# A gated cross-attention block with a SwiGLU layer: the softmax's division moves in front of the turn, onto VectorE, and the loads change order

## What is computed

```python
x = x + tanh(g_xattn[0]) * xattn(ctx, layernorm(x), mask, b)   # 8 heads of 32
x = x + tanh(g_ffn[0]) * ffn(layernorm(x), w_gate, w_up, w_down)

def xattn(memory, query, seq_mask, b):
    Q = split_heads(query) * 32 ** -0.5
    K, V = split_heads(memory[..., :256]), split_heads(memory[..., 256:])
    logits = Q @ K.T + b[0] + -1e30 * (1 - mask)
    return softmax(logits) @ V

def ffn(x, wg, wu, wd):        # weights divided by 127; hidden size 768
    return (silu(x @ wg.T) * (x @ wu.T)) @ wd.T
```

## Time and profile before

| what | value |
|---|---|
| median of 3 runs (lowest, highest) | 141.6 us (140.57, 143.15) |
| span of the profiled execution | 139.7 us |
| PE busy in the span | 129.5 us, 93% |
| DVE busy in the span | 103.4 us, 74% |
| ACT, POOL busy | 90.7 us, 100.3 us |

### The profile page before, as it was taken

One profiled execution on the slowest core, in us unless ns is written; L12 is line 12 of the kernel. 1 busy time (PEld: TensorE's weight loads), 2 busy tenths in 40 slices (PEclk: granted clock), 3 DMA queues, 4 the chain that ended last, 5 costly groups with the idle time before them and its releaser, 6 DMA issues.

```text
span 139.7 us, 3761 instructions
## 1 busy us (share of the span) xinstructions
PE 129.5 (93%) x1276; PEld 98.0 (70%) x1276; DVE 103.4 (74%) x273; ACT 90.7 (65%) x204; POOL 100.3 (72%) x179
## 2 busy tenths in 40 slices
PE   7974998987999999999999999999999999999990
PEld 2324664564566897689779985997667988988870
DVE  4949799977678469787888849878546996676622
ACT  3314599799488877875964889674992556851610
POOL 7463995999999798787788492554697999761530
PEclk9999599999999999999999999999999999999999
DMA  4579990499968930030199106000041062020222
GB/s 139 164 223 359 388 304 9 88 199 195 144 121 155 127 75 0 5 75 5 38 207 195 21 0 150 5 0 0 0 42 38 5 153 77 2 77 2 75 82 89
DMA packets 32033, 14.08 MB, mean 101 GB/s; under 512 B 25588, under 2 KB 31240, under 8 KB 32008
## 3 DMA queue, kind: packets, MB, share of 16 engines
q1 hardware_dynamic: 31968, 13.77, 42.9%
q10 hardware_dynamic: 40, 0.01, 0.1%
HBM read 5.52 MB, written 2.10 MB: 55 GB/s over the span
## 4 chain that ended last, share of the span: by engine, by line
PE 71%; POOL 9%; DMA 7%; DVE 6%; issue 2%; SPq 2%; ACT 0%; POOLq 0%; ACTq 0%; DVEq 0%
PE ps L1426 31%; PE ps L1452 15%; PE ps L1352 4%; DMA x_sb<-in_x_dram 4%; PE ps L1358 4%; PE ps L1328 3%; PE ps L1330 3%; PE ps L1372 3%; PE ps L1283 3%; DMA n_t<-norm 2%; DVE max_cols L1076 2%; POOL rstd L635 2%; POOL q_parts L664 2%; DVE stats L936 2%; PE ps L1212 2%
## 5 line engine op out<-in xcount | busy, mean ns | idle before, releaser
L1426 PE MATMUL ps<-n_t,w_gu_t 128*128 128x256 f16 x384 | 47.7, 273 | 0.5 <-DMA n_t<-norm 0.5
L1426 PEld LDWEIGHTS ps<-n_t,w_gu_t 128*128 128x128 f16 x384 | 36.6, 98 | 6.7 <-DVE h L1131 1.6
L681 POOL TENSOR_TENSOR h<-h 128x256 f16<-128x256 f32 x48 | 31.5, 674 | 11.2 <-ACT h L843 11.2
L1120 DVE SCALAR_TENSOR_TENSOR gated<-tanh_h,ps 128x256 f32<-128x256 f32 x48 | 20.0, 416 | 13.7 <-ACT tanh_h L834 13.5
L834 ACT ACTIVATE tanh_h<-ps 128x256 f32<-128x256 f32 x48 | 18.4, 384 | 15.2 <-PE ps L1426 15.1
L1452 PE MATMUL ps<-w_d_t,h 128*128 128x256 f16 x192 | 24.9, 273 | 0.0
L786 ACT ACTIVATE probs<-ps,exp_bias 128x512 f32<-128x512 f32 x32 | 21.6, 689 | 4.5 <-PE ps L1330 4.1
L1076 DVE TENSOR_REDUCE max_cols<-ps 128x4 f16<-128x512 f32 x32 | 20.7, 683 | 3.8 <-PE ps L1283 3.0
L1131 DVE SCALAR_TENSOR_TENSOR h<-ps,gated 128x256 f32<-128x256 f32 x48 | 20.4, 424 | 2.0 <-DVE gated L1120 0.4
L843 ACT ACTIVATE h<-h 128x256 f16<-128x256 f32 x48 | 18.6, 412 | 2.6 <-DVE h L1131 2.3
L1452 PEld LDWEIGHTS ps<-w_d_t,h 128*128 128x128 f16 x192 | 18.3, 98 | 2.8 <-issue 0.8
(11 more groups left out here) (100 smaller groups left out, 187.3 us busy)
## 6 DMA issues: line engine op xcount, KB each, us to landing
x_sb<-in_x_dram SPq DMA_DIRECT2D x8, 256.0 KB, 8.8
out_dram<-x_sb SPq DMA_DIRECT2D x8, 256.0 KB, 2.3
kv<-in_ctx_dram SPq DMA_DIRECT2D x4, 256.0 KB, 6.5
w_raw<-in_L_ffn_w_gate_dram SPq DMA_DIRECT2D x1, 768.0 KB, 7.8
w_raw<-in_L_ffn_w_up_dram SPq DMA_DIRECT2D x1, 768.0 KB, 9.4
w_raw<-in_L_ffn_w_down_dram SPq DMA_DIRECT2D x1, 768.0 KB, 8.1
q_stacks<-q_parts SPq DMA_TRANSPOSE x12, 3.4
n_t<-norm SPq DMA_TRANSPOSE x7, 3.1
```

Source lines behind the costliest of these rows:

```text
L681: pool.tensor_tensor(h16[:, r % 2, m, 1, :], h32[:, n % NHB, :], h16[:, r % 2, m, 0, :], ALU.subtract).then_inc(h_low, 1)
L1120: mine(dve.scalar_tensor_tensor(out=gated[:, n % 2, :], in0=tanh_h[:, n % 2, :], scalar=1.0, in1=got[:, 0:SH], op0=ALU.add, op1=ALU.mult))
L1426: ins = pe.matmul(dst, lhs, rhs, start=(w == 0 and (k, l) == terms[0]), stop=(k, l) == terms[-1], skip_group_check=True)
```

## The change

Six things are changed together.

1. `wd` multiplies by a 128x32 block of ones instead of `sum_cols`: each head's sum then stands in all 32 rows of its head, one region for one group at a time. `sum_cols` and the POOL instructions that make it go.
2. `oc` moves from ACT to DVE. For each group: a reciprocal of the 128x256 sums, read from PSUM, and a multiplication of the 128x256 values in PSUM with it into `o_sb`, which now holds quotients. `wo` of the next group waits for the multiplication.
3. `at` turns two blocks instead of three; DVE multiplies the turned block by the gate and adds it to `x_sb` in one operation. The reciprocal of 8, the `attn` buffer and the POOL addition go.
4. `var_eps` and `neg_mean` move from POOL to DVE; the statistics of the halves (2,3), (4,5), (6,7) are taken as pairs in the first normalisation.
5. Loads: `x` of the halves 2 and 3 is started before the gates and the weights, and the other loads are mixed differently. Two of three clearing instructions at DVE's start move into the wide program, and two of the small operations for the `exp` bias move to ACT.
6. All five lists of `ORDER` are written anew.

```diff
-        qn2 wn0 qn3 wn1 wn2 nn0 qn4 qn5 nn1 nn2 qn6 fi0 nn3 qn7 nn4 fi1 nn5 nn6 fi2 fi3 fi4 fi5 fi6 fi7""",
+        qn2 qn3 wn0 wn1 nn0 wn2 qn4 nn1 qn5 nn2 nn3 qn6 qn7 nn4 nn5 fi0 fi1 nn6 fi2 fi3 fi4 fi5 fi6 fi7""",
...
-        o_sb = sb("o_sb", [P, 2, NG + 1, SH], F32)
+        o_sb = sb("o_sb", [P, 2, NG, SH], F32)
-        ones32 = sb("ones32", [P, 1], F32)
-        sum_cols = sb("sum_cols", [P, NG, DH], F32)
+        ones32 = sb("ones32", [P, DH], F32)
-        recip = sb("recip", [P, 2, NH], F32)
+        recip = sb("recip", [P, 2, SH], F32)
...
             load_x(sp, 1)
+            load_x(sp, 2)
             load_kv(sp, 1)
+            load_x(sp, 3)
             for n, g in enumerate((g_xattn, g_ffn, attn_b)):
...
-                    elif kind == "attn_t":
-                        n = plan.nth[step]
-                        t = step[1] * QT + step[2]
-                        pool.wait_ge(*plan.emptied(step))
-                        pool.tensor_tensor(x_sb[:, t, :], x_sb[:, t, :], attn[:, n % 2, :],
-                                           ALU.add).then_inc(x1_ready, 1)
...
+                        if which == 2 or norm1_on_pool((step[0].replace("stats", "norm1"), r)):
+                            mine(dve.tensor_scalar(neg_mean[:, at, :], mv[:, at, :, 0], -1.0, None, ALU.mult))
+                        dve.tensor_scalar(var_eps[:, at, :], mv[:, at, :, 1], LN_EPS,
+                                          1.0 / Q_SCALE_SQ if which == 1 else 1.0, ALU.add, ALU.mult
+                                          ).then_inc(var_ready, 1)
...
                     elif kind == "attn_t":
+                        t = step[1] * QT + step[2]
+                        dve.wait_ge(work_filled, plan.filled(step))
+                        dve.scalar_tensor_tensor(out=x_sb[:, t, :], in0=bank32(plan.bank(step))[:, 0:D],
+                                                 scalar=tanh_g[:, 0:1], in1=x_sb[:, t, :],
+                                                 op0=ALU.mult, op1=ALU.add).then_inc(emptied_by["dve"], 1)
+                    elif kind == "o_copy":
+                        dve.wait_ge(weighed, plan.nth[step[0].replace("o_copy", "weigh_d"), b, half, g, LAST] + 1)
+                        dve.reciprocal(recip[:, n % 2, :], sums_at(is_wide)).then_inc(summed_inverse, 1)
...
+                        dve.wait_ge(summed_inverse, n + 1)
+                        dve.tensor_tensor(o_sb[:, (n // NG) % 2, g, :], bank32(O_BANK)[:, 0:SH], recip[:, n % 2, :],
+                                          ALU.mult).then_inc(o_copied, 1)
...
-            for m in (max_cols[:, :, :].rearrange("p t k -> p (t k)"),
-                      bias_rows[:, :, :].rearrange("p c k -> p (c k)"),
-                      max_cols16[:, :, :].rearrange("p t k -> p (t k)")):
-                ins = dve.memset(m.bitcast(F32), 0.0)
-            ins.then_inc(zeros_written, 1)
+            dve.memset(max_cols16[:, :, :].rearrange("p t k -> p (t k)").bitcast(F32), 0.0).then_inc(zeros_written, 1)
...
-                        if first or not values:
-                            before = plan.nth[of("o_copy"), b, half, g]
-                            if values and before:
-                                pe.wait_ge(o_copied, before)
-                            if not values and before > g:
-                                pe.wait_ge(o_copied, before - g)
+                        before = plan.nth[of("o_copy"), b, half, g]
+                        if first and before:
+                            pe.wait_ge(o_copied, before)
...
-                                ins = pe.matmul(sums_at(is_wide)[part, :], sum_cols[:, g, :], pr,
-                                                start=(is_wide and g == 0 and c == 0), stop=(last and g == NG - 1),
+                                ins = pe.matmul(sums_at(is_wide)[part, :], ones32[:, :], pr,
+                                                start=(is_wide and first), stop=last,
...
-                        for g in range(NG + 1):
+                        for g in range(NG):
                             ins = pe.transpose(bank32(n)[:, g * P:(g + 1) * P],
```

More of the change, by code:

```diff
@@ L131, in emptied_by_engine, with stats_of, halves_of @@
     return None
+STATS_PAIRS = {(1, 2): (2, 3), (1, 4): (4, 5), (1, 6): (6, 7)}
+def stats_of(which, r):
+    first = r - r % 2
+    return first if which == 1 and r in STATS_PAIRS.get((1, first), ()) else r
+def halves_of(step):
+    kind, which, r = step
+    return (r,) if kind.startswith(WIDE) else STATS_PAIRS.get((which, r), (r,))
 def norm1_on_pool(step):
@@ L160 @@
[L160 to L164, removed]
@@ L425, in flamingo_block_kernel, with small @@
         plan = Plan(steps + wide, n_early, WORK + HID_BANKS, WORK, emptied_by)
+        norms = [step for e in ("dve", "pool") for step in narrow[e] if step[0] in ("norm1", "norm2")]
+        norms += [step for step in wide if step[0] in (WIDE + "norm1", WIDE + "norm2")]
+        norm_place = {step: i for i, step in enumerate(norms)}
         def ln_slot(kind, which, r):
             pre = WIDE if kind.startswith(WIDE) else ""
[L430 removed]
+            return norm_place[f"{pre}norm{which}", r] % NLB
         def norm_before(kind, which, r):
             pre = WIDE if kind.startswith(WIDE) else ""
[L435 to L436 removed]
+            place = norm_place[f"{pre}norm{which}", r]
+            return None if place < NLB else norms[place - NLB]
+        def small(which, r):
+            return (which - 1) * R + r
         def wait_normed(eng, stats_step):
@@ L449, in wait_norm_used @@
                 return
-            k, w, p = before
+            k, p = before
+            w = int(k[-1])
             if not k.startswith(WIDE):
@@ L724, in run @@
                             act.activation(tanh_g[:, :], gates[:, 0:2], ACT.Tanh).then_inc(tanh_ready, 1)
+                    elif kind == "exp_bias":
+                        act.wait_ge(gates_loaded, 48)
+                        act.wait_ge(shut_out_ready, 1)
+                        act.activation(exp_bias[:, :], exp_bias[:, :], ACT.Identity, scale=MASK_STEP, bias=gates[:, 2:3]
+                                       ).then_inc(shut_out_added, 1)
+                        act.wait_ge(shut_out_added, 1)
+                        act.activation(exp_bias[:, :], exp_bias[:, :], ACT.Relu, scale=-1.0, bias=gates[:, 2:3]
+                                       ).then_inc(shut_out_added, 1)
                     elif kind == "mask_parts":
```

232 lines of the change are left out of this document (95 added, 137 removed).

## The result

The changed kernel takes 159.31 us in the median (158.81 to 160.03, 4 runs) against 141.81 us of the kernel before, measured beside it: a ratio of 1.128 with the interval 1.122 to 1.134. It is slower, by about 17.5 us; predicted were 160 us, with 150 to 170 as the range.

What follows compares the result with a forecast made beforehand. DVE was to replace PE as bound of the attention part: 87.2 us plus 29.6 of reciprocals, 10 idle, 30.9 of PE-bound tail and 1.9 from span to median gave 159.6, say 160 us, range 150 to 170.

Steps and rivals of the forecast that it cites:

- DVE becomes the bound: Attention part: 116.8 us of DVE work before the last multiplication ends, against 106.4, so DVE replaces PE as bound; 75%.
- The price R: Time of one new 128x256 DVE reciprocal: 1.85 us taken, 1.30 to 2.09 kept; sixteen make 29.6 us.
- the scattered places: The old reciprocal's 8 numbers lie scattered, in two pieces; this might excuse 17 ns of its 0.202 us.
- the end at 1.30: Low bound of the reciprocal's price in us, at 4.5 ns a number, if scattered operands explain part of the old cost.
- The page's rule: The skill's reciprocal as iterative division with repeat count 8: 2.28 us per reciprocal, a sum of 167 us.
- The rest of DVE's work: DVE work without reciprocals, up to the end of the last multiplication: 82.2 us before, 87.2 after removals and additions.
- The idle time that stays: DVE idle time up to the last multiplication's end: about 3 us in the head and 7 after it.
- The mark and the tail: End of DVE's last new multiplication at 126.8 us, then 30.9 us bound by PE; span 157.7.
- The cheap reciprocal: Rival: a DVE reciprocal of 256 costs 0.42 us, PE remains the bound, 139 us; 10%.
- The clock: Rival: PE's clock falls while it waits in the attention part; priced at 7 us, 167 us; 7%.
- the waits that go round: Rival: PE stands at `wo` or `at`, then DVE waits for a `tanh` PE must feed; 173 us; 8%.
- The signs: Expected in the profile: DVE busy near 135 us, its row 9, new PE waits, DVE's chain share mostly reciprocals.

Runs made afterwards that it cites:

- experiment 1: Changed kernel with a plain copy in place of the 128x256 reciprocal, so nothing is divided: 138.80 us, 0.987 of the kernel before.
- experiment 3: Changed kernel with a copy in front of the multiplication and a reciprocal nobody reads behind it: 163.04 us, 1.157 of the kernel before.
- experiment 4: Kernel before with only sums spread, divided and added as in the change, old loads and statistics, lists adapted: 175.51 us, 1.235.
- experiment 2: Changed kernel with the reciprocal on the first 128 of 256 columns and a copy on the other 128: 147.29 us, 1.049 of the kernel before.
- experiment 8: Kernel before with the changed kernel's order of the first loads and nothing else: 138.45 us, 0.991 of the kernel before.

## Why the prediction was right

- **DVE becomes the bound.** Right, by experiments 1 and 3. Shortening one DVE operation returns the whole loss; keeping its length and taking it off PE's path returns none.
- **The price R.** 1.85 was taken, from 1.30 to 2.09; it is 1.748, 28.0 us for sixteen where 29.6 was summed. The form of the estimate, a fixed part of 0.149 and 6.6 ns a number, holds: measured are 0.148 and 6.25. The 8 numbers of line 1107 had carried the answer: 0.148 + 8 × 6.25 ns = 0.198 us, and the row says 0.202. So the scattered places explain almost nothing of it, and the end at 1.30 was not needed. On 3 numbers the same line gives 0.167 us, and the row says 0.164.
- **The page's rule.** The Trainium skill ("VectorE: DVE Perf Modes", section "First, the fixed hardware budget") speaks of a repeat count of 8. The trace agrees in direction. The estimate made from it, 2.28 us, was too high: the runs show 6.25 ns a number, six times the 1.04 of other operations and not eight.
- **The rest of DVE's work.** The multiplication took 0.425 us (0.424 taken). The addition took 0.476 instead of 0.424, 0.8 us in all; no run shows why. `neg_mean` took 0.263 instead of 0.164, about 1 us. Lines 994 and 948 grew by 3.4 us, which the sum didn't hold. These errors outweigh the cheaper reciprocal: by line, the durations (mean times count) up to the mark add up to 91.7 us before and 128.6 after, 36.9 more, where the prediction added 34.6. Yet DVE's busy time up to the mark came out under the forecast, 114.7 us against 116.8, because the sum added durations to a busy time. The two differ: a DVE record often starts before the one ahead of it ends, here by 0.07 us, and busy time counts such a stretch once.

```profile
69.55 0.42 DVE L1109 TENSOR_TENSOR o_sb<-ps,recip 128x256 f32<-128x256 f32 x1
69.90 0.41 DVE L1117 SCALAR_TENSOR_TENSOR gated<-tanh_h,ps 128x256 f32<-128x256 f32 x1
```

In all that is about 9.5 us up to the mark before and 14 after. So the close agreement is in part luck: terms that were too small, and an overlap that wasn't thought of.

- **The idle time that stays.** 10.3 us against 10: 3.8 in the head (3 taken) and 6.4 behind it (7). The idea behind it held: a few hundredths between dependent operations and a head that the loads shorten. Experiment 4 shows that the division alone doesn't bring it: with the old loads and statistics and another list, the same DVE work kept 41 us of idle time in the span, against 22.
- **The mark and the tail.** 124.95 against 126.8, and 31.95 us behind it against 30.9. DVE's tail of 20.5 us left PE the bound there. Span 156.9 against 157.7. The profiled run took 158.84 us, 1.9 over its span, as was taken; the median of the four runs lies 0.5 above that run, at 159.3 against 159.6.
- **The rivals.** The cheap reciprocal did not come about, but its time did: experiment 1 has 0.416 us and 138.8 against the 139 worked out. The clock shows one slice of 5 (the kernel before has one too) and a mean of 0.98 from 14.30 us to the mark, so that rival had little. What looks like the waits that go round appears in experiment 4 alone.
- **The signs.** DVE's busy time of 135.2, the slices, the mark, the new waits and the shorter `tanh` wait came as told, though 7.0 us is more than "a few", and DVE's row is full from the second slice and not the fifth. One sign was wrong: of the 49% of the span that DVE holds in the chain, the reciprocals are 13, about a quarter and not most. Here the chain goes through whatever the busy engine does; the reciprocals show in the busy time, and what they cost shows when they are replaced.

## What to carry to other kernels

Before spreading a value so that an operation can be done on full rows, count how many numbers the dear operation then handles: here 8 reciprocals a row became 256, at 6.25 ns each, and the engine that did them became the bound. An engine with idle time takes new work for free at most up to that idle time (24 us here, of which 10 stayed idle), so the sum of its work up to the last dependent step, set against the time at which that step ends now, decides before anything else does. And where each engine's order is written out by hand, a part taken out or put in alone is measured together with a list made for something else.

## What the runs showed of the hardware

Some small DVE operations take two to four times as long in the changed kernel: five of lines 948 and 994, and three of `neg_mean`'s eleven. In each of these cases POOL has an operation on two tensors under way when the DVE operation starts. Timelines of POOL and DVE in the changed kernel:

```profile
17.31 1.16 POOL L685 TENSOR_TENSOR k_parts<-kv,k_parts 128x512 f16<-128x512 f32 x1
...
17.38 1.37 DVE L948 COPY q_parts<-q_parts 128x1024 f16<-128x1024 f16 x1
...
35.70 1.16 POOL L680 TENSOR_TENSOR q_parts<-norm,q_parts 128x512 f16<-128x512 f32 x1
...
35.83 1.31 DVE L994 TENSOR_SCALAR k_parts<-kv 128x512 f16<-128x512 f32 x1
...
49.80 1.16 POOL L680 TENSOR_TENSOR norm<-norm 128x512 f16<-128x512 f32 x1 [2.20 <-ACT norm L731]
...
50.06 1.18 DVE L994 TENSOR_SCALAR k_parts<-kv 128x512 f16<-128x512 f32 x1
```

The copy ends at 18.75, the other two at 37.14 and 51.24: 0.28 us behind POOL's ends at 18.47, 36.86 and 50.96 each time, as if they had waited for POOL and then run. All five lengthened ones of these two lines look so; the seven others take 0.41 to 0.42. Once, in experiment 2, DVE came first: its copy starts at 48.64 and takes 0.42, and POOL's operation that starts at 48.71 takes 1.37 instead of 1.16. The kernel before has such a case too, in the small operation of the earlier trace rows that the prediction took for 1.02 us: it ends at 21.29, and POOL's operation beside it at 21.27. In experiment 8 the same operation takes 0.22.

```profile
20.11 1.16 POOL L664 TENSOR_TENSOR q_parts<-norm,q_parts 128x512 f16<-128x512 f32 x1
```

The Trainium skill says as much ("SBUF — State Buffer", section "SBUF: two separate sides"): a DVE operation in one of its two-port modes and a POOL operation share a pair of ports, and the one that starts second is blocked until the other has ended. The trace agrees with it in these rows, though no view names the mode of a DVE operation, and with an exception: POOL's operation of line 650 on four numbers, from 13.04 to 14.26, lengthened neither of the two that DVE started in it (0.41 each). The runs also show that the price depends on the neighbour: line 994 costs 832 ns in the mean here and 418 in experiments 1 and 2, whose edits are elsewhere. No run moved the POOL operation alone, so the cause rests on these overlaps. The reciprocals and the multiplications out of PSUM did not lengthen.
